# Tensor product stage of a graph network: another order of TensorE's steps in each group's turn

## The reference

```python
s1 = concat([xs[:, :8], xd[:, :8]])                  # 16 scalars of source and destination
v1 = concat([xs[:, 8:], xd[:, 8:]]).reshape(E, 16, 3)
w  = relu(emb @ fc1_w1 / c) @ fc1_w2 / c             # 512 weights per edge
vdot1 = einsum('euk,ek->eu', v1, sh1) / SQRT3        # sh1: the edge's direction
s_t = a1 * (einsum('eu,euw->ew', s1, Wss) + einsum('eu,euw->ew', vdot1, Wvv))
v_t = a1 * (einsum('eu,euw->ew', s1, Wsv)[:, :, None] * sh1[:, None, :] + einsum('euk,euw->ewk', v1, Wvs))
w2 = relu(emb @ fc2_w1 / c) @ fc2_w2 / c             # 384 weights for a second product
scal, gates, vecs = ...                              # the same form again, of s_t, v_t, sh1 and w2
edge_out = concat([tanh(scal), vecs * tanh(gates)]) * norm
return segment_sum(edge_out, edge_dst, num_nodes)
```

## Time and profile before

| | |
|---|---|
| median of 3 runs | 24794.69 us |
| the profiled execution | 24800.48 us |
| its span, first to last instruction | 24798.6 us |
| busy in the span: TensorE / VectorE / ScalarE / GpSimd | 58% / 62% / 21% / 64% |
| stage of the tensor product, in the trace | 18.4 ms to 24.76 ms |
| busy within it, 22000 to 24000 us: TensorE / VectorE / ScalarE / GpSimd | 89% / 88% / 33% / 68% |

### The profile page before, as it was taken

One profiled execution on the slowest core, in us unless ns is written; L12 is line 12 of the kernel. 1 busy time (PEld: TensorE's weight loads), 2 busy tenths in 40 slices (PEclk: granted clock), 3 DMA queues, 4 the chain that ended last, 5 costly groups with the idle time before them and its releaser, 6 DMA issues. The chain is left out here.

```text
span 24798.6 us, 445834 instructions
## 1 busy us (share of the span) xinstructions
PE 14500.5 (58%) x102440; PEld 8927.8 (36%) x102441; DVE 15351.3 (62%) x31597; ACT 5174.1 (21%) x13760; POOL 15792.5 (64%) x16798
## 2 busy tenths in 40 slices
PE   7555555566666669996200000000348888888888
PEld 5444444433334338883100000000333333333333
DVE  9766666665565564444111111299758888888888
ACT  4211111111111114442000000000013333333333
POOL 0377777777777774443477777777126666666665
PEclk9655555555555555555555555555569999999999
DMA  2466666633333334541111111122124433434343
GB/s 66 105 173 172 173 172 173 168 66 68 68 69 68 68 65 148 153 139 36 33 40 40 40 40 40 42 72 72 41 67 110 110 108 108 110 109 110 108 110 99
DMA packets 2469135, 2331.19 MB, mean 94 GB/s; under 512 B 1084287, under 2 KB 1990333, under 8 KB 2465922
## 3 DMA queue, kind: packets, MB, share of 16 engines
q1 hardware_dynamic: 1901630, 1900.27, 27.3%
q0 software_dynamic: 412544, 241.53, 6.2%
q10 hardware_dynamic: 153668, 172.93, 2.8%
HBM read 1765.30 MB, written 537.93 MB: 93 GB/s over the span
## 5 line engine op out<-in xcount | busy, mean ns | idle before, releaser
L768 POOL DMA_INDIRECT rows<-split_table,index x3125 | 2996.8, 959 | 1938.4 <-DMA index<-in_src 1006.5
L2255 POOL DMA_INDIRECT rows_x<-x_table,index x3125 | 2981.1, 954 | 1625.3 <-DMA index<-in_src 771.6
L1648 POOL DMA_INDIRECT rows_dram<-rows,place_now x3125 | 3026.2, 968 | 1487.4 <-issue 951.8
L884 POOL DMA_INDIRECT rows<-x_table,index x3125 | 3280.6, 1050 | 1021.2 <-issue 952.1
L1575 DVE TENSOR_REDUCE rows<-banks 128x108 f32<-128x324 f32 x1250 | 490.7, 434 | 3467.6 <-DMA rows_dram<-rows,place_now 3456.0
L1587 PE MATMUL banks<-row_pieces,hot_turned 128*128 x3125 | 393.8, 290 | 3605.5 <-DVE rows L1575 3542.1
L2371 DVE TENSOR_TENSOR second<-banks,h 128x768 f32<-128x768 f32 x2500 | 1939.9, 818 | 428.2 <-PE banks L2520 428.2
L2363 DVE TENSOR_TENSOR first<-banks,h 128x768 f32<-128x768 f32 x2500 | 1943.8, 821 | 290.3 <-PE banks L2495 278.9
L576 PE MATMUL banks<-counts,low_turned 128*128 128x98 f32 x6250 | 1794.5, 435 | 80.1 <-ACT counts L564 46.1
L576 PEld LDWEIGHTS banks<-counts,low_turned 128*128 128x128 f32 x6250 | 1601.1, 314 | 205.5 <-issue 175.1
L1587 PEld LDWEIGHTS banks<-row_pieces,hot_turned 128*128 128x128 bf16 x3125 | 251.6, 134 | 3747.8 <-issue 3747.8
(11 more groups left out here) (480 smaller groups left out, 34693.3 us busy)
## 6 DMA issues: line engine op xcount, KB each, us to landing
h<-hidden_dram SPq DMA_DIRECT2D x1250, 320.0 KB
acc_moved<-dst_rows SPq DMA_DIRECT2D x625, 320.0 KB
src_row<-in_src_rows SPq DMA_DIRECT2D x625, 320.0 KB
hot_turned<-turned_dram SPq DMA_DIRECT2D x1250, 160.0 KB, 2.2
hot_dram<-onehot SPq DMA_DIRECT2D x625, 160.0 KB
turned_dram<-hot_turned SPq DMA_DIRECT2D x625, 160.0 KB
a_dram<-a ACTq DMA_DIRECT2D x625, 160.0 KB
a<-a_dram SPq DMA_DIRECT2D x625, 160.0 KB, 2.9
```

The costliest lines, as they stand in the source:

```text
L768: nc.gpsimd.indirect_dma_start(out=m["rows"][j][:, t * SPLIT:(t + 1) * SPLIT], out_offset=None, in_=m["split_table"], in_offset=bass.Indir ...
L884: nc.gpsimd.indirect_dma_start(out=m["rows"][j][:, t * C2:t * C2 + F], out_offset=None, in_=m["x_table"], in_offset=bass.IndirectOffsetOnA ...
L1648: nc.gpsimd.indirect_dma_start(out=m["rows_dram"], out_offset=bass.IndirectOffsetOnAxis(ap=m["place_now"][j][:, t:t + 1], axis=0), in_=m[" ...
L2255: nc.gpsimd.indirect_dma_start(out=m["rows_x"][j][:, t * F:(t + 1) * F], out_offset=None, in_=m["x_table"], in_offset=bass.IndirectOffsetO ...
```

## The change

Three calls in `pe_turn` change place. The order in a turn was: turned inputs (second half), return, spread (half 0), unit sums (half 1), words and the branch behind them, own rows, the second branch. It is now: turned inputs, spread (half 0), words and branch, own rows, unit sums (half 1), the second branch, return. The brackets of `pe_close` follow in both. No instruction is added or taken away, and no other engine's code changes.

```diff
             pe_contract(pe, *at(i, j, -1), 1)
         if there(i, j, 1):
             pe_turn_inputs(pe, *at(i, j, 1), 1)
-        if there(i, j, -1):
-            pe_return(pe, *at(i, j, -1))
         if there(i, j, 0):
             pe_spread(pe, i, j, 0)
-            pe_units(pe, i, j, 1)
         if there(i, j, -3) or there(i, j, 2):
             _, n, first_ahead, n_ahead = turn_words(pe, i, j)
         if there(i, j, -3):
             pe_further_visits(pe, *at(i, j, -3), n)
         if there(i, j, 2):
             pe_own(pe, *at(i, j, 2), tile_of(j, k, 2), first_ahead)
+        if there(i, j, 0):
+            pe_units(pe, i, j, 1)
+        if there(i, j, 2):
             pe_own_further(pe, *at(i, j, 2), n_ahead)
+        if there(i, j, -1):
+            pe_return(pe, *at(i, j, -1))
```

## The result

The changed kernel takes 25357.98 us (median of four, 25310.80 to 25368.34); the one before 24795.37 us. The ratio of the runs' means is 1.0223 (95% interval 1.0211 to 1.0235): slower by 563 us. Forecast were 25264 us and a range of 25070 to 25390. The profiled execution has a span of 25366.5 us, 567.9 us above the span before.

The account below looks back on a forecast made before the run. TensorE's order was taken to set the pace, in a loop closing through VectorE. 583 ordinary turns x 0.79 plus 41 loop ends x 0.2 made 469 us, so 25264 us; range 25070 to 25390.

Parts of the forecast that it names:

- Register steps don't pass a matmul that waits: TensorE's sequencer: the word's step can't run before the spread's second pair passes its wait for VectorE, at 22007.6.
- The rule of the Trainium skill: Backs the rival that the sequencer runs ahead of waiting matmuls: own rows 1.1 us sooner, 24708 us; chance 9%.
- The word's step 0.2 us sooner, latency as before: Ahead of the own rows: step at 22007.6 instead of 22007.8, with its 2.05 us to the own rows unchanged.
- The 2.05 us: Time from the word's step (22007.8) to the first own product (22009.87), read in one turn before the change.
- Own rows to brackets 1.59 us instead of 0.60: Unit sums and return now stand there: 0.32, 0.57 and 0.70 us start to start, so +0.99 us.
- An ordinary turn +0.79 us: Sum for a turn without a loop end: -0.2 ahead of the own rows, +0.99 behind; 583 such turns, 461 us.
- Loop ends +0.2 us: At 41 loop ends own rows to brackets go from 4.55 to 4.96 us, less 0.2; 8 us in all.
- The clock: TensorE's granted clock: taken as unchanged, since gaps of about a microsecond don't lower it now.
- its rival: The clock falls in each turn from TensorE's idle time: 412 us on top, 25676 us; chance 3%.
- The idle share of 20%: TensorE would be idle for some 20% of a turn instead of 11%, said in the rival that the clock falls.
- late pieces: Upper bound: GpSimd's pieces late for the node sum by 0.2 us in every turn, 125 us more, 25389 us.
- Costed at nothing: Later unit sums, ScalarE's copy and GpSimd's pieces ahead of the node sum: 0.2 us to spare; uncovered, 0.1 to 0.3 us per turn.

## Why the prediction was right, and what was mis-sized

- **Register steps don't pass a matmul that waits.** Right. It decided the sign, and the rows after show it at the place itself: the step 0.06 us behind VectorE's end. The rule of the Trainium skill (Perfetto Trace Analysis, section Tensor Engine Instruction) that the sequencer is free while a matmul awaits its semaphores doesn't hold for these steps; by it the step would have stood at the turned inputs, which were loaded at 22005.49 in the turn shown.
- **The word's step 0.2 us sooner, latency as before.** Right: 0.06 instead of 0.28 us behind VectorE's end, and a median of 1.89 us from there to the own rows against 1.94. The 2.05 us of the turn that was read are at the long end: by the place of the turn among the 15 of the loop it is 1.78 to 2.09 us in the kernel before.
- **Own rows to brackets 1.59 us instead of 0.60.** Right: 1.57 in the turn shown, a median of 1.58 against 0.60 before.
- **An ordinary turn +0.79 us.** 0.74 measured, from 9.77 to 10.50 (unrounded). The cost behind the own rows is as forecast, 0.98 instead of 0.99; the gain ahead of them is 0.27 us instead of 0.2, from 2.22 to 1.95 between VectorE's end and the own rows.
- **Loop ends +0.2 us.** 14.44 - 14.07 = 0.37. The closing branch itself took 3.84 us (median) instead of 3.62.
- **The clock.** The term that was mis-sized. It was set to nothing, and its rival, with 3%, to a fall in every turn. It fell in between: 120 stretches at the lower level instead of 40. The reason given against it, that gaps of about a microsecond don't do it now, had no row behind it: before, no ordinary turn held an idle time of TensorE over 0.60 us. After, the longest of a turn is 0.86 to 1.17 us. (The idle share of 20% was too high as well: in the 2000 us above it is 13%.) Of the 567 us, 583 x 0.74 = 429 are the order, 41 x 0.37 = 15 the loop ends; 123 are left, and the run with the idle time filled takes 106 of them away. The forecast of 469 us was of the first two, and 444 were measured. That the time lies in the range in spite of the clock is luck: the room up to 25390 was meant for late pieces, which cost nothing, and the clock used it.
- **Costed at nothing.** Right. GpSimd's pieces do come later, but TensorE's array has no idle time ahead of the node sum (22010.80 in the rows above, no bracket). The 0.55 us of its weight loads are no loss: in the kernel before they stood as long, with nothing waited for (the row below). And behind the node sum there is slack, as had been said: the weights of the next spread still wait 0.64 us for VectorE (22011.92).

```profile
22011.47 0.24 PEld L2560 LDWEIGHTS banks<-pieces,hot_half 128*128 128x128 bf16 x5 [0.55 <-issue]
```

One of the stretches at the lower clock, in the timeline of TensorE after, and its busy table:

```profile
22104.73 0.81 PE L2509 MATMUL banks<-first,unit_sum 128*32 128x256 f32 x8
22105.47 1.33 PE L2555 MATMUL banks<-ident,outputs 128*128 128x128 f32 x5
22106.73 1.66 PE L2495 MATMUL banks<-u_turned,w_tensor 32*128 32x384 f32 x8
```

```profile
22104.70:22108.70 4.00, 4.00 (x30) 1.91 (x27) 1.00 (x3) 0.82 (x3) 2.30 (x4) 0.57 0.01 1
```

At 0.57 of full speed, most of it at the lower level of 1.2 GHz, the return takes 1.33 us instead of 0.76 and the brackets 1.66 instead of 0.93. Both stand behind the own rows now, where every delay is paid in full.

## What to carry to other kernels

A register load with a branch behind it was a latency of about 1.8 to 2.1 us on TensorE's sequencer here, counted from the last semaphore wait ahead of it in program order. Loaded ahead of a wait that is there anyway, the word gave back 0.90 us per turn in the changed order and 0.27 in the order before. An operation moved later to fill a gap must not land between the last product that the loop waits for and the operation that the other engine waits for: here 0.27 us per turn were gained ahead of the own rows and 0.98 paid behind them. Idle time on TensorE can cost a second time, through the clock: some 106 of the 567 us here.

## What the runs showed of the hardware

- Four matmuls that use 32 rows of the array each take 0.86 us together, and two of them alone 0.84: they run beside each other (the four start within 0.02 us of one another), and a pair split off saves nothing.
- With a longest idle time of 0.86 to 1.17 us in each ordinary turn, the granted clock fell to half 120 times in the stage, 62 of them not within the 20 us behind a loop end; with 0.30 to 0.60 us it fell 40 times, each at a loop end. Filling the gaps with products that nobody reads took it back to 40, and the kernel became 0.4% faster for it.
- The same register steps take 0.68 to 0.95 us from the branch (L2572) to the first own product in the changed kernel, by the place of the turn among the 15 of the loop, and the kernels differ in it at the same place: the place in the code sets this latency too, and the traces don't say why.
